# Transformer block on one core: y made at the close of the step in front, in banks A0 and A1, and x_in loaded at the head of the queue's step

## What is computed

```python
# layer 0 (layer 1: the same frame without the gates alpha, with rotary q and k and a mask)
y = layernorm(x) * (1 + gamma1) + beta1          # gamma, beta from cond, per sequence
q, k, v = split(y @ qkv_w + qkv_b)               # 16 heads of 16
attn = softmax(q @ k.T * 16 ** -0.5) @ v
x = x + (attn @ proj_w + proj_b) * alpha1
z = layernorm(x) * (1 + gamma2) + beta2
x = x + (gelu(z @ fc1_w + fc1_b) @ fc2_w + fc2_b) * alpha2
```

## Time and profile before

| what | value |
|---|---|
| time of three executions | 1836.41, 1839.49, 1839.64 us (median 1839.49) |
| the profiled execution | 1836.52 us, of which its span 1834.7 us |
| mean granted clock of TensorE | 0.994 |
| TensorE (PE) matmuls busy | 1782.2 us, 97% of the span |
| weight loads (PEld) busy | 1632.8 us, 89% |
| VectorE (DVE) busy | 1245.4 us, 68% |
| ScalarE (ACT) busy | 1229.0 us, 67% |
| GpSimd (POOL) busy | 850.6 us, 46% |

### The profile page before, as it was taken

How to read it: one execution, slowest core, us unless ns; L and a number is a source line. 1 busy time by engine, 2 the same in 40 slices (tenths; PEclk the granted TensorE clock), 3 DMA queues, 4 the chain that set the end, 5 groups by cost and what they waited for, 6 DMA issues and landing times.

```text
span 1834.7 us, 41549 instructions
## 1 busy us (share of the span) xinstructions
PE 1782.2 (97%) x12623; PEld 1632.8 (89%) x12623; DVE 1245.4 (68%) x2985; ACT 1229.0 (67%) x2265; POOL 850.6 (46%) x1036
## 2 busy tenths in 40 slices
PE   7799999999999999999999999999999999999998
PEld 6688999888989888999899999999999999999986
DVE  6777776677676667676687666676766776766751
ACT  4466766766766766777667767667767666767663
POOL 2233434333433433433645556555566555566544
PEclk9899999999999999999999999999999999999999
DMA  6545435445535444554353333333333333332321
GB/s 168 145 111 127 126 90 127 103 114 126 126 97 121 109 109 126 129 134 114 111 161 99 110 85 98 108 97 103 92 102 91 105 101 105 89 110 86 97 72 35
DMA packets 331147, 199.94 MB, mean 109 GB/s; under 512 B 161090, under 2 KB 315716, under 8 KB 331076
## 3 DMA queue, kind: packets, MB, share of 16 engines
q1 hardware_dynamic: 331076, 199.06, 41.0%
HBM read 80.98 MB, written 17.33 MB: 54 GB/s over the span
## 4 chain that ended last, share of the span: by engine, by line
PE 67%; DVE 12%; issue 8%; POOL 5%; SPq 3%; ACT 2%; DMA 2%; POOLq 0%; DVEq 0%; ACTq 0%
PE D L1186 15%; PE C L995 15%; PE B L1142 7%; PE B L995 7%; PE A L1109 6%; PE A L995 5%; PE B L1128 4%; PE E L995 3%; DVE mx L1462 3%; POOL q_flat L657 2%; POOL h_lo L611 2%; PE A L1114 2%; DVE o_sb L1486 1%; DVE exps L1468 1%; DMA rotation<-rotation 1%
## 5 line engine op out<-in xcount | busy, mean ns | idle before, releaser
L611 POOL TENSOR_TENSOR h_lo<-hact,h_hi 128x512 fp32r<-128x512 f32 x256 | 330.7, 1292 | 234.9 <-ACT h_hi L818 221.7
L1186 PE MATMUL D<-wgt_hi,h_hi 128*128 128x256 f32 x1024 | 263.6, 290 | 0.0
L827 ACT COPY probs_turned<-B 128x512 f32<-128x512 f32 x256 | 149.1, 583 | 169.0 <-PE B L1128 169.0
L1109 PE MATMUL A<-k_pad,q_pad 128*128 128x256 f32 x1536 | 256.3, 294 | 5.3 <-DMA q_pad<-q_flat 2.4
L1186 PE MATMUL D<-wgt_lo,h_hi 128*128 128x256 f32 x1024 | 255.7, 282 | 0.0
L1142 PE MATMUL B<-v_blocks,probs_turned 128*128 128x68 f32 x2048 | 254.0, 271 | 1.2 <-ACT probs_turned L827 1.2
L1142 PEld LDWEIGHTS B<-v_blocks,probs_turned 128*128 128x128 f32 x2048 | 248.3, 192 | 6.3 <-ACT probs_turned L827 2.3
L813 ACT ACTIVATE hact<-C,b_col 128x512 f32<-128x512 f32 x256 | 175.7, 686 | 82.7 <-PE C L995 80.4
L1462 DVE TENSOR_REDUCE mx<-A 128x8 f32<-128x512 f32 x256 | 174.3, 681 | 70.5 <-PE A L1114 42.9
L1109 PEld LDWEIGHTS A<-k_pad,q_pad 128*128 128x128 f32 x1536 | 211.2, 191 | 9.5 <-issue 3.2
L822 ACT ACTIVATE exps<-exps 128x512 f32<-128x512 f32 x256 | 161.5, 632 | 86.2 <-DVE exps L1468 83.9
(11 more groups left out here) (141 smaller groups left out, 3869.0 us busy)
## 6 DMA issues: line engine op xcount, KB each, us to landing
k_pad<-k_flat SPq DMA_DIRECT2D x512, 64.0 KB, 2.1
q_pad<-q_flat SPq DMA_DIRECT2D x256, 128.0 KB, 2.3
gates<-gates SPq DMA_DIRECT2D x64, 256.0 KB, 4.4
x_bias<-x_bias SPq DMA_DIRECT2D x32, 512.0 KB, 3.3
rotation<-rotation SPq DMA_DIRECT2D x256, 64.0 KB, 1.9
x_in<-in_x SPq DMA_DIRECT2D x16, 512.0 KB, 4.6
gates<-gated_bias SPq DMA_DIRECT2D x32, 256.0 KB, 4.8
x_res<-in_x SPq DMA_DIRECT2D x16, 512.0 KB, 4.8
```

Of the source, the lines that this page charges most:

```text
L611: pool.tensor_tensor(hb[1][:, m % 2, :], hact[:, m % 2, :], hb[0][:, m % 2, :].bitcast(F32), ALU.subtract).then_inc(h_lo, 1)
L1109: ins = nc.tensor.matmul(dst, qpad[g % 2][:, c, p, b, :, :].rearrange("p x s -> p (x s)"), kpad[g % 2][:, c, q, :, b * S:(b + 1) * S], sta ...
L1186: ins = nc.tensor.matmul(Dk[g // 2][:, (g % 2) * D:(g % 2 + 1) * D], hb[p][:, m % 2, g * P:(g + 1) * P], w_slice(q, W_FF2, D, m, 0, D), st ...
```

## The change

`y_soon(u)` is true for steps -1 and 0 only, so tiles 0 and 1 are made as before. From tile 2 on:

- TensorE: `first_turn(u+2)` stands at the close of step u, between `turn_probs(u, 3, 1)` and `values(u+1, 0)`, and writes A0 and A1, after `subtract(u, 3, b)`. `queries_keys(u+1, 0)` takes the place in mid-step that the turns had. `scores(u, 0, b)` now waits for y_lo of tile u+1.
- VectorE: statistics of x_in before low_qk(0) (layer 1: before sine(0)), aggregates behind low_qk(0) (layer 1: behind cosine(0)); scale and shift where statistics and aggregates stood; y_low as the last of the step.
- GpSimd: `first_rstd` behind hidden_low(2).
- ScalarE: `first_norm` and `first_columns` before exponential(3,0) in layer 0, behind exponential(3,1) in layer 1; the two copies to y_hi at the end of the step, where first_norm stood.
- SyncE: the load of x_in is the first entry of its step.

```diff
-        def y_bank(pair):
-            return (A[0], B[1])[pair]
+        def y_soon(u):
+            return known(u) and u < 1
+        def y_bank(tile, pair):
+            return (A[0], B[1] if known(tile) and tile < 2 else A[1])[pair]
 # SyncE
+            def next_x(u, n):
+                wait_apart(sp, sp_passed, (pe_yt, upto(u + 1, 2, 2)))
+                if n == 1:
+                    wait_apart(sp, sp_passed, (x_stored, upto(u + 2 - NT, 16, 16)))
+                sp.dma_start(x_in, tokens_of(u + 2, n)).then_inc(x_loaded, 16)
             def step(u, n, a, b, c, p):
+                if n is not None and not y_soon(u):
+                    next_x(u, n)
...
-                if n is not None:
-                    wait_apart(sp, sp_passed, (pe_yt, upto(u + 1, 2, 2)))
...
+                if n is not None and y_soon(u):
+                    next_x(u, n)
 # GpSimd
                     hidden_low(u - 1, 2)
+                if n is not None and b is not None:
+                    first_rstd(u + 2)
...
-                if n is not None:
+                if n is not None and b is None:
                     first_rstd(u + 2)
 # ScalarE
-                if a is not None:
+                if y_soon(u):
                     first_high(u + 1, 0)
...
+                if n is not None and b is not None and a == 0:
+                    first_norm(u + 2)
+                    first_columns(u + 2, n)
                 if a == 1:
                     high_qk(u + 1, 1, 0)
...
                     exponential(u, 3, 1)
+                if n is not None and b is not None and a == 1:
+                    first_norm(u + 2)
+                    first_columns(u + 2, n)
...
-                if n is not None:
+                if n is not None and b is None:
                     first_norm(u + 2)
                     first_columns(u + 2, n)
+                elif n is not None:
+                    first_high(u + 2, 0)
+                    first_high(u + 2, 1)
 # TensorE: first_turn, queries_keys, scores
-                if attn is not None:
+                if attn is not None and known(tile) and tile < 2:
                     pe.wait_ge(*((s_sub, upto(tile - 1, 2 * G, 5)), (pv_norm, upto(tile - 1, 2 * G, 4)))[pair])
+                elif attn is not None:
+                    pe.wait_ge(s_sub, upto(tile - 2, 2 * G, 7 + pair))
...
-                elif i == 1:
-                    pe.wait_ge(s_sub, upto(tile - 1, 2 * G, 6))
+                elif i < 2:
+                    pe.wait_ge(s_sub, upto(tile - 1, 2 * G, 5 + i))
...
+                if g == 0 and a is not None and not y_soon(u):
+                    pe.wait_ge(y_lo, upto(u + 1, 2, b + 1))
 # TensorE: step
-                if a is not None:
+                if a is not None and y_soon(u):
                     first_turn(u + 1, 0, b)
                     first_turn(u + 1, 1, b)
+                elif a is not None:
+                    queries_keys(u + 1, a, 0, b)
...
-                if a is not None:
+                if a is not None and y_soon(u):
                     queries_keys(u + 1, a, 0, b)
...
                     turn_probs(u, 3, 1, a)
+                if n is not None and b is not None:
+                    first_turn(u + 2, 0, n)
+                    first_turn(u + 2, 1, n)
                 if a is not None:
                     values(u + 1, a, 0, b)
 # VectorE: step
-                if a is not None:
+                if y_soon(u):
                     y_scale(u + 1, 0)
...
+                if n is not None and b is not None:
+                    first_statistics(u + 2)
                 if a == 0:
                     low_qk(u + 1, 0)
...
+                if n is not None and b is not None and a == 0:
+                    first_aggregate(u + 2)
                 if a == 0:
                     low_qk(u + 1, 1)
...
                     cosine(u + 1, 0)
+                if n is not None and b is not None and a == 1:
+                    first_aggregate(u + 2)
...
-                if n is not None:
+                if n is not None and b is None:
                     first_statistics(u + 2)
                     first_aggregate(u + 2)
+                elif n is not None:
+                    for pair in range(2):
+                        y_scale(u + 2, pair)
+                        y_shift(u + 2, pair)
...
                     second_aggregate(u, 3)
+                if n is not None and b is not None:
+                    y_low(u + 2, 0)
+                    y_low(u + 2, 1)
```

More of the change, by code:

```diff
@@ L506, in step @@
                     sp.dma_start(x1m, x1b).then_inc(x1_moved, 16)
-                if n is not None:
-                    wait_apart(sp, sp_passed, (pe_yt, upto(u + 1, 2, 2)))
-                    if n == 1:
-                        wait_apart(sp, sp_passed, (x_stored, upto(u + 2 - NT, 16, 16)))
-                    sp.dma_start(x_in, tokens_of(u + 2, n)).then_inc(x_loaded, 16)
+                if n is not None and y_soon(u):
+                    next_x(u, n)
                 if b == 0 and not (known(u) and u == 0):
@@ L777, in first_high @@
                 await_(act, pe_v, upto(tile, 2, 0))
-                nc.scalar.copy(pair_of(yb[0], pair), y_bank(pair)[:, :].rearrange("p (c n) -> p c n", c=KC)).then_inc(y_hi, 1)
+                nc.scalar.copy(pair_of(yb[0], pair), y_bank(tile, pair)[:, :].rearrange("p (c n) -> p c n", c=KC)).then_inc(y_hi, 1)
             def second_high(tile, pair):
@@ L911, in step @@
                     high_piece(2, 0, 2)
+                if known(u) and u == NT - 2:
+                    act.wait_ge(mod_done, 32)
+                if n is not None and b is not None and a == 0:
+                    first_norm(u + 2)
+                    first_columns(u + 2, n)
                 if a == 1:
@@ L971, in step @@
                     high_piece(2, 1, 2)
-                if known(u) and u == NT - 2:
-                    act.wait_ge(mod_done, 32)
-                if n is not None:
+                if n is not None and b is None:
                     first_norm(u + 2)
                     first_columns(u + 2, n)
+                elif n is not None:
+                    first_high(u + 2, 0)
+                    first_high(u + 2, 1)
                 if known(u) and u == 0:
@@ L1044, in first_turn @@
                 pe.wait_ge(xn_ready, upto(tile, G, 2 * pair + 2))
-                if attn is not None:
+                if attn is not None and known(tile) and tile < 2:
                     pe.wait_ge(*((s_sub, upto(tile - 1, 2 * G, 5)), (pv_norm, upto(tile - 1, 2 * G, 4)))[pair])
+                elif attn is not None:
+                    pe.wait_ge(s_sub, upto(tile - 2, 2 * G, 7 + pair))
                 for c in range(KC):
                     for g in range(2):
-                        ins = nc.tensor.transpose(y_bank(pair)[:, (2 * c + g) * P:(2 * c + g + 1) * P],
+                        ins = nc.tensor.transpose(y_bank(tile, pair)[:, (2 * c + g) * P:(2 * c + g + 1) * P],
                                                   x_in[:, 2 * pair + g, c * P:(c + 1) * P], ident[:, :])
@@ L1071, in queries_keys @@
                     pe.wait_ge(y_lo, upto(tile, 2, 1))
-                elif attn is None:
+                if attn is None:
                     pass
-                elif i == 1:
-                    pe.wait_ge(s_sub, upto(tile - 1, 2 * G, 6))
+                elif i < 2:
+                    pe.wait_ge(s_sub, upto(tile - 1, 2 * G, 5 + i))
                 else:
@@ L1412, in y_scale @@
             def y_scale(tile, pair):
-                scale_turned(tile, 0, pair, y_bank(pair), pe_yt, mod1_ready, y_scaled)
+                scale_turned(tile, 0, pair, y_bank(tile, pair), pe_yt, mod1_ready, y_scaled)
             def y_shift(tile, pair):
-                shift_turned(tile, 0, pair, y_bank(pair), y_scaled, y_aff)
+                shift_turned(tile, 0, pair, y_bank(tile, pair), y_scaled, y_aff)
             def y_low(tile, pair):
-                low_turned(tile, pair, y_bank(pair), yb, y_hi, y_lo)
+                low_turned(tile, pair, y_bank(tile, pair), yb, y_hi, y_lo)
             def z_scale(tile, pair):
@@ L1649, in step @@
                     cosine(u + 1, 0)
+                if n is not None and b is not None and a == 1:
+                    first_aggregate(u + 2)
+                if a == 1:
                     sine(u + 1, 1)
```

## The result

| | before | after |
|---|---|---|
| median | 1839.84 us (1836.41 to 1840.81, 6 runs) | 1828.44 us (1825.00 to 1831.19, 6 runs) |
| ratio, 95% interval | 1 | 0.9941 (0.9929 to 0.9952) |
| profiled execution, its span | 1836.52, 1834.7 us | 1826.34, 1824.5 us |
| PE busy | 1782.2 us | 1776.8 us |

What follows compares the result with a forecast made beforehand. TensorE's queue was taken to set the step. Gains of 12.3 and 5.2 us less 1.4 and 1.4 give 14.7 us, taking 1838.0 to 1823.3 us, range 1813 to 1834.

Steps and rivals of the forecast that it cites:

- rival 1: Layer 0: y_low and the exponential are each 0.4 us late instead of 0.1, 8.4 us more, 1831.7; chance 0.22.
- Part 1: TensorE mid-step: queries_keys(0) fits in the turns' old wait, saving 1.36; turns at the close cost 0.95; 12.3 us in all.
- Part 2: GpSimd, layer 1: first_rstd no longer delays hidden_low(5), so TensorE saves 0.37 us in 14 steps, 5.2 us.
- Part 3, VectorE and ScalarE: Work moved on these engines is mostly free, but y_low(0) and exponential(3,0) in layer 0 give back 1.4 us each.
- the two thin margins: Layer 0: y_low(0) before scores(0,0), and ScalarE ready before exponential(3,0), both just in time; 0.1 us a step each.
- Part 3, SyncE: The x_in load, moved behind the q_pad loads, has 11 us of quiet queue and delays nothing: free.
- 2: At the close scores(0,0) waits for y_low(0) behind a late y_hi copy, 1.28 us in all 30 steps, 1858.9; chance 0.07.
- The drain of about 1.38 us: Rule against the forecast: each ScalarE table switch adds about 1.38 us, losing 19.3 us, total 1842.6.
- 4: turn_heads, hidden(1) and h_lo wait as much elsewhere and the new order frees nothing, 1838; chance 0.06.
- 3: ScalarE stands 1.28 us more after the table load before exponential(3,0), TensorE waits 17.9 us, 1841.2; chance 0.04.
- 5: Turns at the close cost only 0.72 us and nothing is late, so 24.4 us go, 1813.6; chance 0.07.

Runs made afterwards that it cites:

- qk_old: Changed kernel with queries_keys(0) back at its old, later place and the turns left at the close; 1860.65 us, ratio 1.0123 to the kernel before.
- heads_early: Changed kernel with layer 1's turn_heads(1) put inside queries_keys(0), ahead of its last two matmuls; 1823.52 us, ratio 0.9921 to the kernel before.
- cols: Changed kernel with SyncE's 16 small bias loads of step 1 moved ahead of that step's spreads; 1824.08 us, ratio 0.9930 to the kernel before.
- cols_mods: On top of cols, VectorE's modulations(1,1) in step 0 moved behind low_heads(3); 1820.94 us, ratio 0.9903 to the kernel before.
- act_extra: Changed kernel with one unused ScalarE copy added behind first_columns in layer 0; 1830.61 us, ratio 0.9957 to the kernel before.

## Why the prediction came out as it did

The forecast was 5.1 us too low, with the result inside its range. Of these, 1.8 lie in the base (1838.0 against a median before of 1839.84) and 3.3 in the gain (14.7 against 11.4). The gain was missed twice, with opposite signs: from step 3 on it was 2.8 us larger than the sum, and the start cost some 6 to 7 us for which the sum has no term. That the total came out so near is in part luck. It lies 0.4 above the 1817 to 1828 that the prediction gave its own account, in the room left for rival 1, whose mechanism did not occur. By its steps:

- **Part 1, queries_keys(0) in the wait: right.** The stretch kept its length in both layers, and qk_old shows the 1.36 us to be covered. The turns cost 0.86 instead of 0.95, so the net is 0.50 a step instead of 0.41 (read in layer 0; in layer 1 it is taken to be the same). "1.36 plus turn_heads still start hidden(1) when gelu is done" held too, but the step stopped there: it followed hidden(1) and not ScalarE's copy of the heads, which turn_heads(1) also releases. turn_heads(1) stands 1.40 us behind project(0) where it stood 0.99 behind it, and project(1) loses 0.24 us a step in layer 1. heads_early shows it by giving back 0.24, and qk_old by costing 1.13 and not 1.36 there.
- **Part 2, first_rstd: right.** 0.37 forecast, 0.40 in the run with this part alone. For layer 1 the parts give 0.50 + 0.37 - 0.24 = 0.63, and 0.65 was measured (55.57 to 54.92).
- **Part 3, VectorE and ScalarE: costed too high.** The 1.4 us each for the two thin margins are 0. That both were thin was right: 0.05 and 0.04 us by the added copies. The chain of ScalarE came out at 456.39 against 456.36, as close as the prediction's 451.13 against 451.1 to 451.2. For layer 0 this leaves 0.50 (0.50 measured).
- **Part 3, SyncE: the step that failed.** "11 us of quiet queue ... nothing queues behind its wait" was read from a steady step and taken for all. The number is off already for the steady step: by its own row the q_pad loads end at 458.71 + 2.74 = 461.45, and to 470.21 are 8.8 us. And in step 1 sixteen small loads fill that quiet queue for 10.9 us. Step 2 was 1.3 us longer for it in most profiles and 4.2 in the one shown, where it had been 0.7 longer in the kernel before; cols takes it away.
- **A term that is missing.** The sum counts steps alike from the first on. Step 0 carries modulations and low_pieces on VectorE, has no tile in front to cover its close, and now makes y there as well: 5.1 us later at the mark in the two profiles, 3.2 at equal clock. The new part of it is the wait of 2.4 us for the bare y_low, which is read from the trace and not tested; cols_mods makes up 1.7 at equal clock, largely by shortening a wait that was there before. What the lower clock adds, and why, stays open.

One reading of the earlier trace rows was a little off, and nothing hangs on it: in layer 0 VectorE and ScalarE were free for 31% and 30% of a step, not "a third or more".

The rivals: 1 (margins missed) did not occur; 2 (scores(0,0) waits 1.28 us in every step) occurred in step 0 alone, with 2.4 us, and in no steady step; 3 did not occur: the exponential starts 0.07 us after its table load ends, and that is the subtract's doing. The drain of about 1.38 us that the Trainium skill (ScalarE: Activation LUTs, What ACT_TABLE_LOAD costs) adds to a switch would show here most plainly, in a place without slack: it would lengthen a step of layer 0 by over 1 us (in act_extra 0.29 us of delay at this place cost 0.25), and the step got shorter by 0.5. The trace does not bear it out for this switch. 4 (the stall only moves) is right for 0.24 us in layer 1. 5 (everything goes) came near for layer 0.

## What to carry over

A pipeline's steady step is not the program: when an entry of a queue moves, look at its new neighbours in the first, the second and the turning steps as well, where one-time work stands. When an instruction is put into a wait, list everything that the instruction behind it releases, not only the next matmul; and where that is late, the inserted product can be split around it. A wait that always lasts is room for work, and its length can be read directly by taking the filler out.

## What the runs showed of the hardware

- A wait of TensorE of 2.83 us at 159.46 was followed, 0.7 us later, by 3.4 us at a granted clock of 0.50, the 1.2 GHz level; waits of 1.1 to 1.4 us at the same place were not. The step with both was 4.2 us longer than a steady one. Nearly the same start-up code put the mark anywhere from 91.4 to 95.7 us in seven profiles, with a mean granted clock up to there between 0.93 and 0.86. The steady steps of one profile repeat within some 0.06 us. Effects of a few us are therefore read from step lengths here, and from totals only with an interval.
- Four transposes in a row cost 0.36 us, eight more in the same stream 0.86, somewhat over 0.1 each.
- An added instruction can cost less than its row: a ScalarE copy of 0.40 us held back the next instruction by 0.29, a VectorE copy of 0.26 us by 0.18.
- The small loads of biases stand some 0.64 us apart in SyncE's queue: sixteen are 10.9 us, four times the 2.7 us in which the same queue issues its four q_pad spreads.
